# The rows of FFN 7 transposed by DRAM scratch and VectorE, and moved steps on VectorE, ScalarE and GpSimd

## The reference

```python
x = x + 0.5 * ffn(layernorm(x))
x = x + attn(layernorm(x))
x = x + 0.5 * ffn(layernorm(x))

def ffn(x):                       # x as (2, 2048, 256); x_prev is x one token earlier, zero at the start
    xr = mu_r * x + (1 - mu_r) * x_prev
    xk = mu_k * x + (1 - mu_k) * x_prev
    return sigmoid(xr @ W_r.T) * (square(relu(xk @ W_k.T)) @ W_v.T)

def attn(x):                      # 16 heads of 16 features, no softmax, no mask
    q, k, v, u = relu(x @ Wq.T) / 4, relu(x @ Wk.T) / 4, x @ Wv.T, silu(x @ Wu.T)
    out = q @ (k.T @ v)           # per head; k.T @ v sums over all 2048 tokens
    return (srms_norm(out) * u) @ Wo.T     # srms_norm: divide by the root mean square of a head
```

## Time and profile before

| what | before |
|---|---|
| median of 3 runs (lowest to highest) | 307.89 us (307.72 to 310.2) |
| the profiled execution, its span | 307.94 us, 306.2 us |
| TensorE (PE) busy | 298.5 us, 97% |
| VectorE (DVE) busy | 247.4 us, 81% |
| ScalarE (ACT) busy | 235.5 us, 77% |
| GpSimd (POOL) busy | 214.5 us, 70% |
| granted clock of TensorE in all 40 slices | 9 or more tenths |
| store to `spread`, 256 KB, median to landing | 4.5 us |
| load from it, 256 KB, median to landing | 2.7 us |

### The profile page before, as it was taken

How to read it: one execution, slowest core, us unless ns; L and a number is a source line. 1 busy time by engine, 2 the same in 40 slices (tenths; PEclk the granted TensorE clock), 3 DMA queues, 4 the chain that set the end, 5 groups by cost and what they waited for, 6 DMA issues and landing times.

```text
span 306.2 us, 5777 instructions
## 1 busy us (share of the span) xinstructions
PE 298.5 (97%) x2003; PEld 271.7 (89%) x2003; DVE 247.4 (81%) x601; ACT 235.5 (77%) x461; POOL 214.5 (70%) x237
## 2 busy tenths in 40 slices
PE   6999999999999999999999999999999999999995
PEld 4888879978988898998988998999999999999894
DVE  4899896677876966985993798596989798999695
ACT  3988949969779779689178368489797979699981
POOL 4598969779689489479168116736797979759823
PEclk9999999999999999999999999999999999999999
DMA  7950070070330510000000000000001101001123
GB/s 234 382 208 2 2 137 2 2 137 0 58 83 0 80 59 0 2 1 2 0 2 1 2 0 0 2 2 2 0 16 56 37 34 54 17 2 68 42 99 137
DMA packets 28416, 15.05 MB, mean 49 GB/s; under 512 B 17122, under 2 KB 27364, under 8 KB 28388
## 3 DMA queue, kind: packets, MB, share of 16 engines
q1 hardware_dynamic: 28096, 14.42, 16.7%
q10 hardware_dynamic: 292, 0.26, 0.2%
HBM read 8.39 MB, written 6.29 MB: 48 GB/s over the span
## 4 chain that ended last, share of the span: by engine, by line
PE 63%; DVE 16%; POOL 8%; ACT 7%; issue 3%; DMA 1%; ACTq 0%; DVEq 0%; POOLq 0%
PE psK L1328 6%; PE psX L1328 6%; PE psK L1330 6%; PE psK L1329 6%; PE psX L1330 6%; PE psX L1329 6%; PE psRV L1328 5%; PE psRV L1330 5%; PE psRV L1329 5%; DVE mix L978 3%; PE psA L1533 2%; PE psX L1546 2%; PE psK L1533 2%; PE psA L1345 2%; DVE gate L1054 2%
## 5 line engine op out<-in xcount | busy, mean ns | idle before, releaser
L978 DVE SCALAR_TENSOR_TENSOR mix<-psA,mu,mix 128x512 f32<-128x512 f32 x60 | 41.5, 744 | 10.0 <-ACT mix L663 10.0
L454 POOL TENSOR_TENSOR mix_k_lo<-mix,mix_k_hi 128x512 fp32r<-128x512 f32 x26 | 33.6, 1313 | 5.1 <-ACT mix_k_hi L696 5.1
L663 ACT ACTIVATE mix<-psA,one_mu 128x511 f32<-128x511 f32 x60 | 36.9, 697 | 0.0
L1328 PE MATMUL psRV<-ffn_hi,mix_r_hi 128*128 128x256 f32 x120 | 34.3, 286 | 0.0
L1330 PE MATMUL psRV<-ffn_hi,mix_r_lo 128*128 128x256 f32 x120 | 33.6, 280 | 0.0
L1329 PE MATMUL psRV<-ffn_lo,mix_r_hi 128*128 128x256 f32 x120 | 33.5, 279 | 0.0
L646 ACT ACTIVATE xn<-xs,shiftA,rstdA 128x256 f32<-128x256 f32 x53 | 27.9, 623 | 2.6 <-POOL shiftA L438 2.6
L1328 PE MATMUL psRV<-ffn_hi,act_hi 128*128 128x256 f32 x96 | 27.6, 287 | 0.2 <-POOL act_lo L476 0.2
L1330 PE MATMUL psRV<-ffn_hi,act_lo 128*128 128x256 f32 x96 | 26.8, 279 | 0.0
L1329 PE MATMUL psRV<-ffn_lo,act_hi 128*128 128x256 f32 x96 | 26.8, 279 | 0.0
L947 DVE BATCH_NORM_STATS2 statsA<-xs 128x6 f32<-128x256 f32 x64 | 22.4, 412 | 2.7 <-DMA xs<-x_dram 2.6
(11 more groups left out here) (211 smaller groups left out, 1086.5 us busy)
## 6 DMA issues: line engine op xcount, KB each, us to landing
xs<-x_dram SPq DMA_DIRECT2D x7, 512.0 KB, 7.8
out_dram<-xs SPq DMA_DIRECT2D x7, 512.0 KB, 2.8
spread<-xn SPq DMA_DIRECT2D x8, 256.0 KB, 4.5
squares<-spread SPq DMA_DIRECT2D x8, 256.0 KB, 2.7
out_dram<-xs SPq DMA_DIRECT2D x4, 128.0 KB, 1.7
xs<-x_dram ACTq DMA_DIRECT2D x2, 128.0 KB, 3.1
xs<-x_dram SPq DMA_DIRECT2D x2, 128.0 KB, 2.8
silu_u<-w_ffn_k_dram SPq DMA_DIRECT2D x1, 256.0 KB, 4.0
```

Of the source, the lines that this page charges most:

```text
L454: nc.gpsimd.tensor_tensor(mix_k_lo[:, h, :], mix[:, 0, h, :], mix_k_hi[:, h, :].bitcast(F32), ALU.subtract).then_inc(s_lo_k, 1)
L663: nc.scalar.activation(mix[:, rk, h, 1:BLOCK], psA[:, h, 0:BLOCK - 1], ACT.Copy, scale=one_mu[:, rk, h:h + 1]).then_inc(s_prev, 1)
L978: nc.vector.scalar_tensor_tensor(out=m, in0=psA[:, h, :], scalar=mu[:, rk, h:h + 1], in1=m, op0=ALU.mult, op1=ALU.add).then_inc(s_mix, 1)
L1328: nc.tensor.matmul(dst, a_hi, b_hi, start=start, stop=False)
```

## The change

FFN 7 joins the turned ones, with its rows loaded into `wsum`. ScalarE writes the normalised rows of turned FFNs in the order of the scratch, so that the store takes runs of 128 elements instead of 32. One square of FFN 1 goes from GpSimd to ScalarE. `wo_hi` and `wo_lo` come earlier in block 2. On GpSimd `act_low(6)` comes ahead of `norm_second(0)`. On VectorE `keep_g` comes ahead of `r_low` in every block; in block 5 only the sums of heads 0 are left, followed by the turn of 7; their Newton steps and scaling come in block 6, between `x2_low(5)` and `mix_current(7)`.

```diff
@@ -295,11 +295,21 @@
 
             return mix_part(n, rk, h) + n
 
-        TURNED = range(3, 7)
+        TURNED = range(3, 8)
         QUAD = 32
         QUADS = P // QUAD
-        quads = squares[:].rearrange("p g e -> p (g e)")
+
+        def quads_of(n):
+
+            return (squares[:].rearrange("p g e -> p (g e)") if n < 7
+                    else wsum[:].rearrange("p n e -> p (n e)"))
+
         spread = nc.dram_tensor("spread", [len(TURNED), 2, QUADS, P, P], F32).ap()
+
+        def spread_rows(t):
+
+            return xn[:].rearrange("p t d -> p (t d)").rearrange("p (g j t h f) -> p g t h j f", g=2, j=QUADS, t=2, h=HALVES
+                                                                 )[:, t // 2, t % 2, :, :, :]
 
         def half(g):
             return slice(g * D, (g + 1) * D)
@@ -387,14 +397,16 @@
                 for g in range(2):
 
                     sp.wait_ge(*normalized(n, 2 * g + 1))
-                    sp.dma_start(spread[k, g].rearrange("j p (q f) -> p q j f", f=QUAD),
-                                 xn[:, 2 * g:2 * g + 2, :].rearrange("p t (h j f) -> p (t h) j f", h=HALVES, j=QUADS)
+                    sp.dma_start(spread[k, g].rearrange("j p e -> p j e"),
+                                 xn[:, 2 * g:2 * g + 2, :].rearrange("p t d -> p (t d)").rearrange("p (j e) -> p j e", j=QUADS)
                                  ).then_inc(s_spread[g], 16)
                 if k > 0:
                     sp.wait_ge(s_tA, 2 * n)
+                if n == 7:
+                    sp.wait_ge(s_wmean, 4)
                 for g in range(2):
                     sp.wait_ge(s_spread[g], 16 * (k + 1))
-                    sp.dma_start(quads[:, g * BANK:(g + 1) * BANK],
+                    sp.dma_start(quads_of(n)[:, g * BANK:(g + 1) * BANK],
                                  spread[k, g].rearrange("j (c i) e -> (j c) (i e)", i=QUADS)).then_inc(s_quads[g], 16)
             for b in range(NB - 1):
                 store_x(b)
@@ -463,6 +475,8 @@
 
             def act_squares(n):
                 for h in range(HALVES):
+                    if (n, h) == (1, 1):
+                        continue
                     pool.wait_ge(s_act_hi, parts(n) + h + 1)
                     nc.gpsimd.tensor_tensor(act_k[:, h, :], act_k[:, h, :], act_k[:, h, :],
                                             ALU.mult).then_inc(s_sq, 1)
@@ -472,7 +486,10 @@
                     act_squares(n)
                 for h in range(HALVES):
 
-                    pool.wait_ge(s_sq, parts(n) + h + 1)
+                    if (n, h) == (1, 1):
+                        pool.wait_ge(s_act_first, HALVES + 1)
+                    else:
+                        pool.wait_ge(s_sq, parts(n) + h + 1 - (n > 1))
                     nc.gpsimd.tensor_tensor(act_lo[:, h, :], act_k[:, h, :], act_hi[:, h, :].bitcast(F32),
                                             ALU.subtract).then_inc(s_act_lo, 1)
 
@@ -564,15 +581,15 @@
                 k_low(i + 1)
                 if i > 1:
                     kt_low(i - 1)
+                if i == 2:
+                    pool.wait_ge(s_wo_hi, 1)
+                    nc.gpsimd.tensor_tensor(wo_lo[:], wo[:], wo_hi[:].bitcast(F32), ALU.subtract).then_inc(s_wo_lo, 1)
                 scales_b(i)
                 x1_low(i)
                 if i == 1:
                     weight_sum("v")
-                if i == 2:
-                    pool.wait_ge(s_wo_hi, 1)
-                    nc.gpsimd.tensor_tensor(wo_lo[:], wo[:], wo_hi[:].bitcast(F32), ALU.subtract).then_inc(s_wo_lo, 1)
+            act_low(6)
             norm_second(0)
-            act_low(6)
             k_low(7)
             kt_low(5)
             scales_b(6)
@@ -643,7 +660,10 @@
                 for t in tiles:
                     if t in xn_vector.get(n, ()):
                         continue
-                    nc.scalar.activation(xn[:, t, :], tile_row(xs, b, t), ACT.Identity,
+                    given, rows = tile_row(xs, b, t), xn[:, t, :]
+                    if n in TURNED:
+                        given, rows = given.rearrange("p (h j f) -> p h j f", h=HALVES, j=QUADS), spread_rows(t)
+                    nc.scalar.activation(rows, given, ACT.Identity,
                                          bias=shiftA[:, t:t + 1], scale=rstdA[:, t:t + 1]).then_inc(s_xn, 1)
 
             def first_column(n):
@@ -711,6 +731,9 @@
                     if n > 1 and h == 0:
                         act.wait_ge(s_v, 2 * n)
                     nc.scalar.activation(act_hi[:, h, :], act_k[:, h, :], ACT.Square).then_inc(s_act_hi, 1)
+                    if (n, h) == (1, 1):
+                        act.wait_ge(s_act_hi, HALVES)
+                        nc.scalar.activation(act_k[:, h, :], act_k[:, h, :], ACT.Square).then_inc(s_act_first, 1)
 
             def activate_k2(n):
                 for h in range(HALVES):
@@ -842,10 +865,10 @@
                     normalize(i + 2)
                 if i >= 5:
                     square_heads(i - 5)
-                x1_high(i)
                 if i == 2:
                     act.wait_ge(s_w_in["o"], 16)
                     nc.scalar.activation(wo_hi[:], wo[:], ACT.Identity).then_inc(s_wo_hi, 1)
+                x1_high(i)
                 relu_q(i - 1)
 
             front(7, None, 6)
@@ -982,7 +1005,7 @@
                 for s, v in free:
                     dve.wait_ge(s, v)
                 dve.wait_ge(s_halo, n + 1)
-                blocks = quads.rearrange("p (g i t h f) -> p g h t i f", g=2, i=QUADS, t=2, h=HALVES)
+                blocks = quads_of(n).rearrange("p (g i t h f) -> p g h t i f", g=2, i=QUADS, t=2, h=HALVES)
                 for g in range(2):
                     dve.wait_ge(s_quads[g], 16 * (n - TURNED[0] + 1))
                     for h in range(HALVES):
@@ -1229,6 +1252,8 @@
                     turn(i + 1, {4: [(s_wcen, 4)], 5: [(s_kvbd, 1)]}.get(i, ()))
                 if i > 1:
                     x2_low(i - 1)
+                if i == 6:
+                    head_norms(0, True)
                 mix_current(i + 1)
                 if i == 1:
                     stats_a(3)
@@ -1242,17 +1267,22 @@
                 if i == 6:
                     add_attention(0)
                 stats_b(i)
+                keep_g(i - 1)
                 r_low(i + 1)
                 if i == 3:
                     center_weight("v", 4)
-                keep_g(i - 1)
                 if i == 4:
                     mask_kv(0)
                 if i == 6:
                     stats_a(8)
                 if i >= 5:
                     gate_heads(i - 5)
-                    head_norms(i - 5)
+                if i == 5:
+                    for g in range(2):
+                        head_sums(0, g)
+                    turn(7, [(s_gu, 2)])
+                elif i == 6:
+                    head_norms(1)
 
             x2_low(6)
             projections(6)
@@ -1634,7 +1664,6 @@
             q_of(4, (s_silu, 18))
 
             ffn_k(6, [(s_gacc, 5)])
-            transpose_a(7, [(s_gu, 2)])
             transpose_b(5)
             ffn_r(6)
             k_and_u(5)
```

## The result

| | before | after |
|---|---|---|
| median of 9 runs each | 309.42 us | 310.44 us |
| lowest to highest | 307.48 to 310.2 | 310.16 to 312.15 |
| profiled execution, span | 307.94, 306.2 us | 311.32, 309.6 us |
| mean granted clock of TensorE in the profile | 1.0 | 0.989 |

The changed kernel is slower: ratio 1.0073, 95% interval 1.0045 to 1.0101. The times of every kernel here fall in two groups some 1.8 us apart, which come from the opening, so where single microseconds matter I compare the faster groups: about 307.8 before, 310.16 to 310.44 after, **+2.5 us**.

A forecast was written before the change was run, and what follows sets the result against it. The prediction took holes in TensorE's stream of matmuls to decide the time. Holes -1.87, transposes -0.87 and a new stand +4.1 gave +1.4 us on 307.94, so 309.3 us, range 305.2 to 311.4.

The forecast's parts named there:

- The gains: On TensorE, time saved by closing five holes (1.87 us) and removing FFN 7's transposes (0.87 us).
- the holes: Five places up to 160 us where TensorE's matmul starts lie too far apart; closing them gains 1.87 us.
- the transposes: Eight TensorE transposes of FFN 7 leave TensorE's stream, a gain of 0.87 us.
- rival D: The two parts that hang on GpSimd bring nothing: +2.3, 310.2 us; counted with the forecast, together 0.46.
- The stand: TensorE waits ahead of transpose_g(0) for silu(5, 1), delayed by the moved Newton steps: 4.1 us.
- The hold of L1156 and its follower: GpSimd's two act_lo hold VectorE's first Newton step until 136.3 and the step behind it until 137.8.
- Rival A: Nothing holds the Newton steps; TensorE stands 2.4 us, sum -0.3, 307.6 us; chance 0.20.
- Rival B: TensorE's wait at transpose_g(0) does not form, only the gains stand: -2.7, 305.2 us; chance 0.15.
- C: TensorE's clock falls to half rate in the new stand, costing 2.3 us more: 311.6 us; chance 0.13.

The follow-up runs named there:

- e6: The changed kernel without FFN 7's turn, with the Newton steps and GpSimd's order as before: 305.95 us, ratio 0.9924.
- e9: e4 run once more, beside e10: 306.81 us, ratio 0.9931.
- e10: e6 run once more, beside e9 on the same chip: 306.75 us, ratio 0.9943.
- e3: The changed kernel with GpSimd's order as before, norm_second(0) ahead of act_low(6): 309.81 us, ratio 1.0032.
- e1: The changed kernel with 14 extra matmuls of 512 columns, results unread, ahead of transpose_g(0): 308.87 us, ratio 1.0031.
- e2: The changed kernel with 30 extra 128x128 transposes, results unread, ahead of transpose_g(0): 309.11 us, ratio 1.0034.
- e8: The changed kernel with 7 extra matmuls of 512 columns, results unread, ahead of transpose_g(0): 310.33 us, ratio 1.0063.
- e7: The kernel before with only the Newton steps and scaling moved behind x2_low(5) and act_low(6) ahead of norm_second(0): 311.54 us, ratio 1.0113.
- e5: The changed kernel with the Newton steps and scaling right behind turn(7), act_low(6) still first on GpSimd: 310.15 us, ratio 1.0042.
- e4: The changed kernel with the Newton steps and scaling right behind turn(7), and GpSimd's order as before: 305.03 us, ratio 0.99.

## Why the prediction failed

**The gains** were right: the holes 1.87 forecast, 2.01 in the trace and 1.9 to 2.0 alone (e6); the transposes 0.87, seen in the trace and, freed of the stand, 0.7 in e9 against e10. Nothing of GpSimd's chain came late, so rival D is out.

**The stand** was right in place, order and nearly in size: 3.69 against 4.1. Part of the difference is an addition: seven steps of 0.26 and the 0.69 behind 137.8 end at 140.31, not 140.55, so by its own terms the prediction had a stand of 3.9 and 309.1 us. On the forecast's scale, with the opening's 0.25 and the holes' 1.87 taken off, L1159 was to be let go at 135.7 and mix_current(7) to start at 138.43; they came at 135.35 and 137.80, that is 0.63 early: 0.33 at L1159, 0.24 by the addition, the rest in the steps. TensorE was ready 0.15 earlier as well, which leaves 0.4 to 0.5 of difference. The hold of L1156 and its follower is shown by e3. Rival A names a kernel that exists: it is e3 with the clock held, 307.46 and 307.71. Rival B did not come.

**The step that failed** is in the paragraph on the numbers: C was put as a case beside the forecast, with a chance of 0.13. It is no alternative to the stand but follows from it, and in 16 of 16 executions. Given a stand of 4 us and an opening that ran at the lower level after TensorE had done nothing, the forecast should have carried the fall in its sum. The sum in order: -2.0 (holes) -0.87 (transposes) +3.7 (stand) is +0.8; with 1.5 for the clock and the 0.26 that e1 still loses behind the stand it is +2.6, and +2.5 was measured. C's price, 2.3 with at least 1.5, was near: 1.5 in most executions and 2.6 in the profiled one. Its 311.6 came out high by 0.4 in the stand and 0.8 in the clock. The number, 309.3, was 1.1 below the median and the range held it; what was wrong is that I took no measurable change for likeliest, where the interval lies wholly above 1.

Is it the stand's length that decides? Hardly alone, since one kernel shows both. It never fell in e1 and e2, with less than 0.5 us left. With 2.1, 2.18, 2.83 and 3.25 us (e8, e3, e7, e5; lengths from one profile each) both occurred: it fell in 5 of 12, 9 of 12, 3 of 6 and 5 of 11 executions. With 3.69 it always fell. e5 fell less often than e3 although it stands longer, but at another place in the stream and on another chip, and the counts are small; what decides within this range stays open. By the Trainium skill, page "TensorE: Matmul & The Clock Gate", section "Why this matters for your kernels", idle gaps between bursts bring the half rate back. These runs agree in that: in 16 of 16 executions with 3.69 us, in 22 of 41 with 2.1 to 3.25.

## What to carry to other kernels

Price a new stand of TensorE together with the clock it costs: here 1.5 us on top of 3.7, and with a stand of 2.1 us it already happened in 5 of 12 executions. When small dependent vector steps are moved, look for a gap of VectorE in which GpSimd is idle too, and follow what is queued behind them to the engine that sets the end; a gap further ahead (e4) turned 2.5 us of loss into 2.8 of gain by moving two calls. A gain ahead of a stand is lost in the stand: the transposes' 0.87 showed in the time only once the stand was gone.

## What the runs showed of the hardware beyond the rows before

- A step of one input and constants (L1159, TENSOR_SCALAR on 64 elements) is held by GpSimd's operation as well: 1.20 us against 0.20 without it. The prediction had counted on this, with a row only for L1133, which has two inputs.
- A chain of dependent steps does not lose once but each time GpSimd gets its next operation in: 0.94, 1.00, 1.23 and 1.66 us where 0.23 and 0.69 were due (e5).
- The opening comes in two lengths with the same work. Its 16 matmuls of 256 columns take 3.69 us in the profile of before and 5.52 in that of e3, with a granted clock of 1.00 recorded in both; that is the 1.8 us between the two groups of times. In all five profiles of the slower group these 16 take 4.9 to 5.6 us, in the eight others 3.69. What makes them slow was not tested.
- The clock can fall while TensorE is busy again: in e3 it was still 2.4 GHz in the transposes behind the stand (1.09 us for eight) and fell in the matmuls after them.
